# RWKV macaron layer on eight cores: the second FFN's first half moved behind the next tile's attention front

## The reference

```python
x = x + 0.5 * ffn(layernorm(x))
x = x + attn(layernorm(x))
x = x + 0.5 * ffn(layernorm(x))
# ffn: xr, xk = mixes of token t and token t-1
r = sigmoid(xr @ W_r.T); k = square(relu(xk @ W_k.T))
out = r * (k @ W_v.T)
# attn (RWKV): k, v, r = xk @ Wk.T, xv @ Wv.T, sigmoid(xr @ Wr.T)
# wkv: per head a decaying sum over earlier tokens of exp(k)*v, over that of exp(k)
out = (r * wkv(k, v, time_decay, time_first)) @ Wo.T
```

## Time and profile before

| what | value |
|---|---|
| median of two runs | 3712.8 us (3710.05 and 3715.56) |
| the profiled execution | 3713.76 us |
| span in its profile, core 0, the slowest | 3712.2 us |
| spans of the eight cores | 3703.3 to 3712.2 us |
| PE, matmuls | 1789.4 us busy, 48% of the span |
| DVE | 1582.9 us busy, 43% |
| ACT | 771.2 us busy, 21% |
| granted TensorE clock, mean, core 0 | 0.735 of full speed |

### The profile page before, as it was taken

One profiled execution on the slowest core, in us unless ns is written; L12 is line 12 of the kernel. 1 busy time (PEld: TensorE's weight loads), 2 busy tenths in 40 slices (PEclk: granted clock), 3 DMA queues, 4 the chain that ended last, 5 costly groups with the idle time before them and its releaser, 6 DMA issues.

```text
span 3712.2 us, 26572 instructions; the slowest of 8 cores (3703.3 to 3712.2 us)
## 1 busy us (share of the span) xinstructions
PE 1789.4 (48%) x7192; PEld 770.8 (21%) x7192; DVE 1582.9 (43%) x3754; ACT 771.2 (21%) x1222; POOL 6.5 (0%) x11
## 2 busy tenths in 40 slices
PE   2454545544544445455444444454554545444544
PEld 1121212222222212122222222121222212221222
DVE  1444444444434444444444444444444444444443
ACT  1222221221222222212212212222122222222211
POOL 0000000000000000000000000000000000000000
PEclk9777767777777777777776777776777767777767
DMA  9000000000000000000000000000000000000000
GB/s 162 15 12 12 1 12 12 12 12 7 6 12 12 12 12 0 12 12 12 12 6 6 12 12 12 12 1 12 12 12 12 1 12 12 12 12 12 1 6 12
DMA packets 18224, 50.07 MB, mean 13 GB/s; under 512 B 2593, under 2 KB 2722, under 8 KB 18082
## 3 DMA queue, kind: packets, MB, share of 16 engines
q0 software_dynamic: 7280, 14.68, 2.6%
q1 hardware_dynamic: 6194, 16.92, 1.4%
q10 hardware_dynamic: 4608, 16.78, 1.1%
HBM read 46.27 MB, written 16.78 MB: 17 GB/s over the span
## 4 chain that ended last, share of the span: by engine, by line
PE 47%; DVE 18%; ACT 13%; DVEq 9%; issue 9%; ACTq 3%; DMA 1%; POOL 0%; POOLq 0%
PE p L368 21%; PE p L370 19%; DVEq L353 5%; PE p L310 3%; ACT junk L246 3%; PE p L505 2%; DVE s1F L253 2%; PE p L502 2%; DVE dbuf L339 2%; ACT ka_fm L423 2%; ACT zfF L321 2%; DVE z_tmF L286 1%; DMA fwvt_s<-fwvt 1%; DVEq L529 1%; DVE numb L523 1%
## 5 line engine op out<-in xcount | busy, mean ns | idle before, releaser
L368 PE MATMUL p<-fwvt_s,ka_fm 128*128 128x512 bf16 x512 | 266.4, 520 | 442.2 <-ACTq L424 442.2
L368 PE MATMUL p<-fwrt_s,xr 128*128 128x512 bf16 x512 | 279.4, 546 | 316.5 <-DVEq L353 316.5
L310 PE MATMUL p<-idb_s,z_tmF 128*128 128x128 bf16 x512 | 64.7, 306 | 538.3 <-DVEq L288 538.3
L370 PE MATMUL p<-fwrt_s,xr 128*128 128x512 bf16 x512 | 274.0, 535 | 0.0
L370 PE MATMUL p<-fwvt_s,ka_fm 128*128 128x512 bf16 x512 | 261.8, 511 | 0.0
L430 DVE TENSOR_TENSOR u_sb<-recbF,p 128x512 f32<-128x512 f32 x64 | 44.0, 688 | 464.1 <-PE p L370 459.5
L368 PE MATMUL p<-fwkt_s,xk 128*128 128x512 bf16 x512 | 193.8, 379 | 93.3 <-ACTq L390 93.3
L368 PE MATMUL p<-wkt_s,xk 128*128 128x512 bf16 x256 | 140.4, 548 | 161.2 <-DVEq L353 161.2
L246 ACT ACTIVATE junk<-R 128x1024 bf16<-128x1024 f32 x96 | 101.4, 1056 | 520.8 <-DVEq L434 297.1
L370 PE MATMUL p<-fwkt_s,xk 128*128 128x512 bf16 x512 | 193.9, 379 | 0.0
L395 DVE TENSOR_SCALAR denb<-esig 128x1024 f32<-128x1024 f32 x64 | 44.4, 694 | 322.7 <-ACTq L390 322.7
(11 more groups left out here) (114 smaller groups left out, 3132.5 us busy)
## 6 DMA issues: line engine op xcount, KB each, us to landing
R<-x SPq DMA_DIRECT2D x32, 512.0 KB, 3.3
out<-R ACTq DMA_DIRECT2D x32, 512.0 KB, 2.6
fwrt_s<-fwrt POOLq DMA_DIRECT2D x1, 2048.0 KB, 21.5
fwkt_s<-fwkt POOLq DMA_DIRECT2D x1, 2048.0 KB, 37.6
fwvt_s<-fwvt POOLq DMA_DIRECT2D x1, 2048.0 KB, 49.4
wkt_s<-wkt POOLq DMA_DIRECT2D x1, 2048.0 KB, 61.3
wvt_s<-wvt POOLq DMA_DIRECT2D x1, 2048.0 KB, 73.3
wrt_s<-wrt POOLq DMA_DIRECT2D x1, 2048.0 KB, 86.1
```

Source lines behind the costliest of these rows:

```text
L310: last = t.transpose(p0bank[:, cc * 128:(cc + 1) * 128], src[:, cc * 128:(cc + 1) * 128], idb[:])
L368: t.matmul(pa[:], lhsbuf[:, cc * 128:(cc + 1) * 128], wv[:, cc, 0:512], start=st, stop=sp)
L370: last = t.matmul(pb[:], lhsbuf[:, cc * 128:(cc + 1) * 128], wv[:, cc, 512:1024], start=st, stop=sp)
```

## The change

Two calls in the loop change places. `attn_a` of tile i+1 now comes before `ffn_a` of F2 of tile i, and so `ffn_b` of F2 follows directly on its `ffn_a`, in every iteration. No instruction is added, removed or altered, and the event that each step waits for is the same step's as before. It applies in the 31 iterations that have a next tile (i from 0 to 30).

```diff
             rA = attn_d(i, Rb[i % 3], evg)
-            st_f2 = ffn_a(i, Rb[i % 3], "F2", r_ev=rA, s1_ev=None)
             if i + 1 < n_tiles:
                 st_a[i + 1] = attn_a(i + 1, Rb[(i + 1) % 3],
                                      r_ev=rF1[i + 1], s1_ev=None)
+            st_f2 = ffn_a(i, Rb[i % 3], "F2", r_ev=rA, s1_ev=None)
             rF2 = ffn_b(i, Rb[i % 3], *st_f2, nslot="F2")
             store(i, rF2)
```

## The result

The changed kernel takes 3744.1 us (median of 11 runs) against 3716.0 us (median of 10) for the kernel before, which is 28 us or 0.8% more, where 3694 us was forecast. The ratio is 1.0103, with a 95% interval of 1.0061 to 1.0144: a small loss, clear of no change, and within the 2% that the prediction took as its mark for "faster" or "slower". (Runs in which one die of the chip ran slower than the other are left out of all ratios here; in some experiments they are so many that the plain median lies above the ratio.)

A forecast was written before the change was run, and what follows sets the result against it. No engine is full; the kernel is one long relay, bound by its links and hand-overs. From 3713.8 us, seams +14.6 and bursts -34.1 gave 3694 us, range 3658 to 3745.

The forecast's parts named there:

- The seams: Three hand-overs per iteration, 4.00 us before and 4.47 after: +0.47 us an iteration, +14.6 us over 31.
- The second and the third: End of recbA to F2's L253, forecast 1.54 us; end of ka_tm to the start of fwvt, forecast 2.78 us.
- The burst term: TensorE's bursts fwrt, wkt and fwvt: -1.10 us an iteration, all from fwrt, -34.1 us over 31; called the weakest term.
- These three are the bursts that get new predecessors: Only F2's fwrt, wkt and fwvt, taking 6.29, 5.89 and 5.71 us, were taken to have new neighbours.
- the one row of fwrt: Ahead of the loop, fwrt with its new neighbours takes 5.19 us, 1.10 us less than its mean; taken as its forecast.
- a period outside 112.3 to 114.7 us: Sign that the prediction is wrong: the loop's period in the changed profile leaves this range.
- The iterations are regular: Loop timeline: 3413.29 us in 30 periods, read as 113.8 us each.
- periods repeat: Argument that neighbours set the bursts' rate, used against one row being only a draw.
- the burst term averages out: Rival: fwrt's single row is a draw, so only the seams' +14.6 us remain: 3728 us, chance 0.24.
- TensorE keeps the low level longer: Rival: more PE idleness in F2 puts fwrt, wkt and fwvt at their long ends: 3779 us, chance 0.12.
- fwvt at the high level: Rival: short idle stretches keep the clock up, so fwvt takes 3.71 us, 2.00 less: 3632 us, chance 0.06.
- the rule that I had put beside this rival: Trainium skill, HAM oscillation: the clock falls back when idle gaps grow too long; shorter gaps keep it up.

The follow-up runs named there:

- the two filled kernels: The kernel before and the changed kernel, each with dummy matmuls in TensorE's idle stretches: 3368.4 us and 3383.7 us.
- fill_before: The kernel before with dummy matmuls, which nobody reads, in TensorE's idle stretches: 3368.4 us, ratio 0.907 to the kernel before.

## Why the prediction was wrong

**The seams: right.** Forecast +0.47 us a period, measured +0.45 in the trace and +0.46 in the two filled kernels, where the clock is high. I had 0.15, 1.54 and 2.78 us, and they are 0.26, 1.56 and 2.70. The second and the third were read from rows that already had the new neighbours; the first was taken from another in-order start.

**The burst term: wrong, in sign.** The step that failed is "These three are the bursts that get new predecessors", by which the other bursts were left out of the sum at nothing, and with it the term of -1.10 us, priced by the one row of fwrt. Against 6.29, 5.89 and 5.71 us, fwrt took 5.72, wkt 5.90 and fwvt 5.87: -0.40 us together where -1.10 were forecast. The bursts whose neighbours had not changed were the ones that lost: fwrt of F1 went from 5.44 to 5.53 us, wkv from 5.42 to 5.68 (to the first L513), fwvt of F1 from 5.93 to 6.40 (to gfm), +0.81 us together. So all bursts gave +0.41 us a period, where I had -1.10. With +0.45 for the seams and under 0.1 for the rest that is the +0.93 measured. (These compare the slowest cores, 0 and 4. The means over all eight cores give the same: +0.89 us a period, of which the bursts are +0.41.) The error is 1.5 us, 31 times: 47 us, all but a few of the 50 us between 3694 and 3744. The sign of being wrong that I had named, a period outside 112.3 to 114.7 us, came true by 0.01 us, with 114.71.

**Why one row misled me.** The misreading began at "The iterations are regular": 113.8 us was a mean of 30 periods that were themselves 112.5 to 116.2 us long, and "periods repeat" was then my argument against the rival of the average. I had read that a burst's length is set by its neighbours, and took 5.19 us from the one row with the right ones. The row's value came true in the long periods, and was no gain. A burst begins at 1.2 GHz and goes over to 2.4 GHz at a moment that isn't tied to its own start (3.0 to 5.3 us after it in the windows above), so a start that is a little later can lose less time at the low level, and the next burst begins in another position. What one burst saves, another can pay, and only the sum over all six of a period is worth anything. The Trainium skill (TensorE: Matmul & The Clock Gate, What's actually happening) says that the window in which TensorE's activity is watched runs freely, and that the same kernel shows different numbers of slow matmuls; the rows agree, with fwrt at 5.19 and 6.27 us in one execution. I had cited that page's warning and given it 0.24.

**The rivals.** The nearest was "the burst term averages out", 3728 us: right in sign, and 16 us short. "TensorE keeps the low level longer", 3779 us, named the right mechanism in the wrong bursts, and too large. fwvt at the high level did not happen: it took 5.20 to 6.66 us, although PE's idle stretches ahead of it were only 2.4 and 1.7 us in every iteration. So the rule that I had put beside this rival, read gap by gap, doesn't hold here.

**What stays open.** Why the changed order falls into the long period more often than the order before isn't derived: the runs show that half a microsecond on the path undoes it, and not why. That the moments of the clock's rise are what holds the periods at a few values fits all runs and is argued from them; no run moves those moments alone. Also open is why four cores begin in the short period and four in the long one with the same program.

## What to carry to other kernels

If a kernel's chain is a relay between engines and TensorE's granted clock is between 0.5 and 1, look at the lengths of single periods and not at their mean. Where they cluster, a change of under a microsecond a period can't be judged by its time alone: compare the two versions with TensorE kept busy too, where the difference in the order shows as it is (15 us here, not 28). Read the cost of a new seam from a place where the same neighbours already meet, such as the first or last iteration, but never price one burst by one row. And before exchanging whole blocks of a relay, take the layer norms and copies off the path, which was worth 17% here, and fill the idle stretches with matmuls that nobody reads, which was worth 9%.

## What the runs showed of the hardware that I had not expected

- Useless work can make a kernel faster: 256 columns more on DVE, 32 times, took 26 us off the changed kernel (3744.1 to 3718.2).
- All eight cores could run dummy matmuls in nearly every idle stretch, PE 85% busy, at a mean granted clock of 0.987 to 0.989 (fill_before). The low clock of both kernels (0.735 and 0.719 at 48% and 47% busy) thus came with idleness and not with load.
- Most periods take one of few values, 112.6, 114.3, 116.0 and at times 117.8 us, in kernels whose work on the path differs by 0.5 to 0.9 us, and 109.2 appears when 3.6 us of it are taken away. From the seventh period on, all eight cores of the changed kernel go through the same sequence of them.
